# Reordering the set-up of a count-matrix build, and giving one half of an fp16 split to another engine

## The reference

```python
h = relu(layernorm(x)); x = x + L0(h)   # 4-head attention over the edges, segment sums by src
h = relu(layernorm(x)); x = x + L1(h)   # relu(h @ Wv + bv) * gamma, summed by dst
h = relu(layernorm(x)); x = x + L2(h)   # (h + pi * segment_sum(h[src], dst)) @ W.T + b
h = relu(layernorm(x)); x = x + L3(h)   # three Chebyshev filters, softmax mix, batch norm, relu
```

## Time and profile before

| | before |
|---|---|
| median of 3 runs | 1038.48 us (1036.12 to 1039.69) |
| profiled execution, own time | 1036.59 us |
| its span | 1034.8 us |
| mean granted TensorE clock | 0.973 |
| PE busy | 939.5 us (91%) |
| DVE busy | 855.0 us (83%) |
| ACT busy | 601.0 us (58%) |
| POOL busy | 530.0 us (51%) |

### The profile page before, as it was taken

How to read it: one execution, slowest core, us unless ns; L and a number is a source line. 1 busy time by engine, 2 the same in 40 slices (tenths; PEclk the granted TensorE clock), 3 DMA queues, 4 the chain that set the end, 5 groups by cost and what they waited for, 6 DMA issues and landing times.

```text
span 1034.8 us, 21453 instructions
## 1 busy us (share of the span) xinstructions
PE 939.5 (91%) x8293; PEld 563.3 (54%) x8293; DVE 855.0 (83%) x1296; ACT 601.0 (58%) x826; POOL 530.0 (51%) x522
## 2 busy tenths in 40 slices
PE   3787778888896999999999999999999999999995
PEld 2544445455462223232323333335699999999884
DVE  8899999999774999999999999999976745533466
ACT  8576677878546998989989898881100000001233
POOL 7788568575003999999999999870000000000000
PEclk9999998999896999999999999999999999999996
DMA  0010000000236122122222222230001100010211
GB/s 10 27 37 10 6 7 26 6 11 2 55 123 182 43 56 58 41 66 50 49 62 57 67 59 66 64 87 1 1 33 40 44 24 11 1 42 9 79 36 46
DMA packets 98577, 43.82 MB, mean 42 GB/s; under 512 B 85004, under 2 KB 96652, under 8 KB 98352
## 3 DMA queue, kind: packets, MB, share of 16 engines
q1 hardware_dynamic: 96784, 40.74, 15.0%
q0 software_dynamic: 1696, 1.74, 0.7%
HBM read 30.03 MB, written 12.41 MB: 41 GB/s over the span
## 4 chain that ended last, share of the span: by engine, by line
PE 66%; DVE 21%; issue 5%; ACT 3%; POOL 2%; DMA 2%; SPq 0%; DVEq 0%; ACTq 0%; POOLq 0%
PE PS L1322 20%; PE PS L1077 14%; PE PS L1087 12%; DVE oneS L410 7%; DVE mov L410 6%; PE PS L1820 4%; PE PS L1066 3%; PE PS L547 3%; PE PS L539 3%; ACT Eb L1134 2%; POOL Eb L977 1%; PE PS L1330 1%; PE PS L876 1%; DVE Eb L1151 1%; PE PS L1806 1%
## 5 line engine op out<-in xcount | busy, mean ns | idle before, releaser
L1151 DVE TENSOR_TENSOR Eb<-Eb,PS 128x2048 f32<-128x2048 f32 (+4 forms) x175 | 342.2, 2014 | 20.6 <-POOL Eb L977 10.6
L1134 ACT ACTIVATE Eb<-PS,small 128x1024 f32<-128x1024 f32 (+4 forms) x350 | 333.6, 1004 | 41.7 <-PE PS L1077 36.6
L977 POOL TENSOR_SCALAR Eb<-Eb 128x1024 f32<-128x1024 f32 (+4 forms) x350 | 318.9, 934 | 73.9 <-ACT Eb L1134 70.5
L1322 PE MATMUL PS<-hs,CT 128*128 128x192 f16 (+1 forms) x2500 | 212.5, 246 | 0.1
L583 ACT ACTIVATE CT<-PS 128x500 f32 x313 | 175.7, 586 | 62.7 <-PE PS L547 60.8
L1322 PEld LDWEIGHTS PS<-hs,CT 128*128 128x128 f16 (+1 forms) x2500 | 206.6, 98 | 3.2 <-issue 0.6
L1077 PE MATMUL PS<-Qb,Kb 96*128 96x512 f16 (+3 forms) x700 | 180.8, 362 | 9.7 <-DMA Kb<-kd 6.2
L1087 PE MATMUL PS<-Eb,V 128*25 128x512 f32 (+3 forms) x1400 | 167.5, 551 | 0.9 <-DVE Eb L1151 0.8
L539 PE MATMUL PS<-mov,oneS 128*128 128x100 f16 x1565 | 127.6, 214 | 40.0 <-DVE mov L410 31.8
L539 PEld LDWEIGHTS PS<-mov,oneS 128*128 128x128 f16 x1565 | 96.2, 101 | 97.8 <-DVE mov L410 52.4
L1077 PEld LDWEIGHTS PS<-Qb,Kb 96*128 96x128 f16 (+1 forms) x700 | 42.5, 98 | 195.4 <-ACT Eb L1134 185.3
(11 more groups left out here) (282 smaller groups left out, 904.3 us busy)
## 6 DMA issues: line engine op xcount, KB each, us to landing
Kb<-kd SPq DMA_DIRECT2D x168, 96.0 KB, 2.4
qd<-QH SPq DMA_DIRECT2D x12, 192.0 KB, 2.5
kd<-QH SPq DMA_DIRECT2D x12, 192.0 KB, 3.4
hs<-t_d SPq DMA_DIRECT2D x12, 192.0 KB, 2.5
Qb<-qd SPq DMA_DIRECT2D x4, 384.0 KB, 3.8
CT<-x_d SPq DMA_DIRECT2D x1, 1200.0 KB, 8.1
x_d<-B SPq DMA_DIRECT2D x6, 192.0 KB, 1.8
t_d<-A SPq DMA_DIRECT2D x6, 192.0 KB, 1.9
```

The lines of the kernel that those rows point to most:

```text
L977: g.tensor_scalar(e, e, EHI, ELO, ALU.min, ALU.max).then_inc(S("clamped"), 1)
L1134: a.activation(e, ps, ACT.Exp, scale=K.unsc[0:r, :]).then_inc(S("score_exp"), 1)
L1151: v.tensor_tensor(e, e, cn, ALU.mult).then_inc(S("weighed"), 1)
L1322: m = p.matmul(bank(t % FIRST)[0:r, 0:w], K.CT[:, a, 128 * t:128 * t + r], hs[:, a, :, :].rearrange("p k d -> p (k d)"), start=(a == 0), s ...
```

## The change

In the build: POOL no longer makes the slot numbers beyond the first block (L203 is gone). DVE makes them instead from the first 120 columns, by adding a constant (`more_slots`): for block 1 and blocks 2 to 3 ahead of the wait for `item0`, for blocks 4 to 7 behind `turnW`, for blocks 8 to 13 at set 1. `slots(0)` stands ahead of the `turnW` instructions. The zeros are shared anew: 1,800 and 9,000 columns on POOL, 6,500 on DVE, 14,500 and 7,550 on ACT. POOL's second piece stands ahead of `gather(1)`, and DVE's ahead of `slots(1)`. PE turns the first keys after the sums of blocks 1 to 3, ahead of those of blocks 4 to 7. The third part's comparisons move from sets 0 and 1 to sets 1 and 2, its sums from set 2 to set 3. `high(2)` moves from set 7 to set 5.

In L1: the high half is made by ACT, as a copy with a scale, behind `lin_copy(g + 1)` in its stream. The low half stays on DVE and moves out of `l1_d(g)` to behind `l1_a(g + 2)`.

```diff
-HIGH_AT = {3 if j == 1 else 6 * (j - 1) + 1: j for j in range(1, NJ)}
+HIGH_AT = {(3, 5)[j - 1] if j < 3 else 6 * (j - 1) + 1: j for j in range(1, NJ)}
...
-PAST_AT = {0: (0, 1, 2, 3), 1: (4, 5, 6)}
-SUM_AT, SLOTS_AT, TABLE_AT = 2, 5, 7
+PAST_AT = {1: (0, 1, 2, 3), 2: (4, 5, 6)}
+SUM_AT, SLOTS_AT, TABLE_AT = 3, 5, 7
...
-ZG1, ZG2 = 3500, 10500
-ZV = ZG2 + 4500
-ZA = ZV + 18500
+ZG1 = 1800
+ZG2 = ZG1 + 9000
+ZV = ZG2 + 6500
+ZA = ZV + 14500
+ZEROED = 5
...  build_gpsimd
-    g.iota(K.iotaS[:, BLOCK:SLOTS], [[GI, 12 * (NJ - 1)], [LH, 2], [1, GI]], base=GI * 12, channel_multiplier=0,
-           allow_small_or_imprecise_dtypes=True).then_inc(S("iota"), 1)
...
     keys(0)
+    g.memset(K.CTf[:, ZG1:ZG2], 0.0).then_inc(S("zero"), 1)
     g.wait_ge(S("slot_w"), 2)
     gather(1)
-    g.memset(K.CTf[:, ZG1:ZG2], 0.0).then_inc(S("zero"), 1)
...  build_vector
+    def more_slots(a, b):
+
+        v.wait_ge(step, own.n)
+        v.tensor_scalar(K.iotaS[:, BLOCK * a:BLOCK * b], K.iotaS[:, 0:BLOCK * (b - a)], float(12 * GI * a), None, ALU.add
+                        ).then_inc(step, own.up())
+
+    more_slots(1, 2)
+    more_slots(2, 4)
     v.wait_ge(S("item0"), 1)
...
         passes(0, t)
+    slots(0)
     v.wait_ge(S("identf"), 1)
...
-    slots(0)
-    v.wait_ge(S("iota"), 6)
+    K.turn_at = own.n
+    more_slots(4, 8)
     v.wait_ge(S("passed"), 1)
+    v.wait_ge(step, own.n)
...
     high(0)
+    v.memset(K.CTf[:, ZG2:ZV], 0.0).then_inc(S("zero"), 1)
     slots(1)
-    v.memset(K.CTf[:, ZG2:ZV], 0.0).then_inc(S("zero"), 1)
     table(0)
...
+        if s == 1:
+            more_slots(8, NJ)
+            v.wait_ge(step, own.n)
         if s in HIGH_AT:
...  build_tensor
     sums(0)
+    t.wait_ge(K.own["v"].sem, K.turn_at)
     windows(0)
-    sums(1)
+    sums(1, last=4)
     turn_items(0)
+    sums(1, first=4)
     windows(1)
...  prop_scalar
             lin_copy(g + 1, tiles(g + 1))
+        a.wait_ge(S("h2"), g + 1)
+        a.activation(K.HP[0][:, 4 * g:4 * g + tiles(g), 0, :], K.A[:, 4 * g:4 * g + tiles(g), :], ACT.Copy, scale=UP
+                     ).then_inc(S("hi"), 1)
...  prop_vector
-        v.wait_ge(S("h2"), g + 1)
-        split(A[:, 4 * g:4 * g + n, :], 0, g)
+
+    def l1_e(g):
+
+        n = tiles(g)
+        o = [K.HP[0][:, 4 * g:4 * g + n, i, :] for i in range(2)]
+        v.wait_ge(S("hi"), NJ + g + 1)
+        v.scalar_tensor_tensor(out=o[1], in0=A[:, 4 * g:4 * g + n, :], scalar=UP, in1=o[0], op0=ALU.mult, op1=ALU.subtract
+                               ).then_inc(S("split_l2"), 1)
...
         if g + 1 < NG:
             l1_a(g + 1)
+        if g:
+            l1_e(g - 1)
         l1_c(g)
         if g + 1 < NG:
             l1_b(g + 1)
         l1_d(g)
+    l1_e(NG - 1)
     degrees()
```

More of the change, by code:

```diff
@@ L425, in build_vector @@
     high(0)
+    v.memset(K.CTf[:, ZG2:ZV], 0.0).then_inc(S("zero"), 1)
     slots(1)
-    v.memset(K.CTf[:, ZG2:ZV], 0.0).then_inc(S("zero"), 1)
     table(0)
+    v.wait_ge(S("iota"), 5)
     soft = softmax_pieces(v, K)
@@ L483, in build_tensor, with sums @@
     t.matmul(bank(5)[0:BLOCK, 0:1], K.row0[:, :], K.onef[:, :], start=True, stop=True).then_inc(S("item0"), 1)
-    def sums(h):
+    def sums(h, first=0, last=NJ):
         a, b = PARTS[h]
-        for j in range(a, b):
+        for j in range(max(a, first), min(b, last)):
             for t_ in range(7):
@@ L492, in sums @@
                              start=(t_ == 0), stop=(t_ == 6))
-        m.then_inc(S("passed"), 1)
+        if b <= last:
+            m.then_inc(S("passed"), 1)
     def windows(h):
@@ L520, in build_tensor @@
     sums(0)
+    t.wait_ge(K.own["v"].sem, K.turn_at)
     windows(0)
-    sums(1)
+    sums(1, last=4)
     turn_items(0)
+    sums(1, first=4)
     windows(1)
     t.wait_ge(S("identb"), 1)
-    t.wait_ge(S("zero"), 5)
+    t.wait_ge(S("zero"), ZEROED)
     PE = mybir.EngineType.PE
@@ L576, in build_scalar @@
     a.activation(K.CTf[:, ZA:ZT], K.zf[:, 0:1].to_broadcast([128, ZT - ZA]), ACT.Copy).then_inc(S("zero"), 1)
-    a.wait_ge(S("zero"), 5)
+    a.wait_ge(S("zero"), ZEROED)
     for i, g in enumerate(PRESENT):
```

## The result

The changed kernel takes 1031.97 us (median of 5 runs, 1030.93 to 1032.83), the kernel before 1038.48 (5 runs, 1034.37 to 1039.69). The ratio is 0.9946, 95% interval 0.9933 to 0.9959: 5.6 us faster, between 4.3 and 7.0 (the two medians differ by 6.5). The forecast was 1030.4 within 1026.5 to 1034.5. In a second set of runs the same kernel had 1031.19 against 1038.53, ratio 0.9932 (0.9919 to 0.9946): 7.1 us, between 5.6 and 8.4.

A forecast was written before the change was run, and what follows sets the result against it. The prediction saw no single bound: PE carried 66% of the chain of waits, DVE 21%. Set-up 6.5 us plus L1 0.9 made 7.4 us, taken from a mean of 1037.7 for a forecast of 1030.4, range 1026.5 to 1034.5.

The forecast's parts named there:

- The head and the zeros: Set-up: without the iota and with zeros shared anew, PE's first set starts at 23.7 against 30.49, 6.8 us earlier.
- The 0.6 us that this would have cost here: Set-up head: by the skill's rule, more_slots held for POOL's short instructions would make the gain 0.6 us smaller.
- Sets 2 to 11: Build, stepped set by set: set 6 starts at 42.8 to 43.4 against 48.75, a gain of 5.4 to 5.9 us.
- my rival on the faster side: Set-up: the clock does not fall after the sums and fewer hold-ups spare the sets: 10 us, 1027.8; chance 0.10.
- The step that failed: Third block's keys before set 12: ready in time with high(2) at about 40, so DVE's wait goes: + 0.43 us.
- my first rival: Set-up's gain lost before set 12, by block 1's late keys among others: 4.2 us gain, 1033.5; chance 0.14.
- All sets alike from set 12 on: Build from set 12: nothing differs, and DVE's pace carries the 6.5 us lead to the build's end.
- my rival on the slower side: Build: PE's clock stays at the lower level, PE becomes the bound, net 10.3 us slower, 1048; chance 0.03.
- a lead that shrinks there: Sign of being wrong: the set-up's lead, forecast at 6.5 us, shrinks in the sets after 12.
- L1: High half moved to ACT closes PE's idle times at the second and fourth group: 0.39 + 0.52 = 0.9 us.
- One sign that I had named for being wrong: L1: ACT's new copy ends what DVE waits for; gain 0 if DVE waits each time as long as it saved.
- the 1.6 us slower stage: L1 priced by the longer ACT instruction alone, seven times 0.23 us: stage 1.6 us slower, whole gain 4.9.

The follow-up runs named there:

- Experiment 8: POOL's long iota replaced by DVE's additions alone, on the kernel before, with order and shares of zeros as before: 1033.59 us, ratio 0.9969.
- Experiment 11: The changed kernel with the old shares of zeros on POOL, DVE and ACT: 1030.43 us, ratio 0.9934 to the kernel before.
- experiment 5: The changed kernel with L1's high halves back on DVE, so the new set-up alone: 1031.62 us, ratio 0.9944 to the kernel before.
- Experiment 3: The changed kernel with POOL's keys(2) ahead of gather(3): 1028.66 us, ratio 0.9917 to the kernel before.
- Experiment 2: The changed kernel with high(2) back after set 7: 1031.74 us, ratio 0.9943 to the kernel before.
- experiment 4: The changed kernel with the third block's keys turned by PE after set 10 in place of set 9: 1029.69 us, ratio 0.9918 to the kernel before.
- experiment 6: L1's high halves on ACT alone, on the kernel before, with its build unchanged: 1035.79 us, ratio 0.9985.
- 10: The changed kernel with keys(2) ahead of gather(3) and high(2) back after set 7: 1029.56 us, ratio 0.9929 to the kernel before.
- 12: The changed kernel with one-element DVE memsets behind the one-hot instructions of sets 7 to 10: 1031.78 us, ratio 0.9948 to the kernel before.
- 7: high(2) after set 5 in place of set 7, alone, on the kernel before: 1036.41 us, ratio 0.9991.
- experiment 9: The changed kernel with keys(2) ahead of gather(3) and 22 more POOL comparisons from the fourth block on: 1030.44 us, ratio 0.9933 to the kernel before.

## Why the prediction was right, and where it was wrong

The total was right within its range: 7.4 us of gain forecast, 5.6 (4.3 to 7.0) measured in one set of runs and 7.1 (5.6 to 8.4) in the other. Part of that is luck. At set 6 the gain was larger than forecast (6.1 to 7.0 in three profiles, against 5.4 to 5.9), from there to set 12 the late keys took more back than forecast (3.4 to 6.3 left, against 6.5), and the two errors offset each other. (The sum itself is 0.1 off: 1037.7 less 7.4 is 1030.3.)

**The head and the zeros: right.** `lw` at 0.17 us, keys(0) ending at 14.34 (forecast 14.9), the last zeros at 22.05 (22.6), PE 1.08 us later at 23.13 (23.7). Experiment 8 shows the iota's part by itself: 4.83 us at `cI`. Experiment 11 shows that the last zeros, and not the one-hots, start PE. `lw` started at 2.96, before my own 3.3, since both `more_slots` (0.45 us together, from 1.89) fit into DVE's wait for `item0`. The Trainium skill (SBUF — State Buffer, Who interferes with whom) has a `tensor_scalar` in a two-port mode and a GpSimd instruction shut each other out. The 0.6 us that this would have cost here, by the prediction, did not come: POOL's short instructions, of 0.2 to 0.3 us, did not hold these two. The trace agrees with that rule at the comparisons of part 1. As forecast, they were held beside POOL's short memset: 4.87 us in place of 2.54, with their end at 11.46, where I had 11. It cost nothing here, and 1 us in experiment 8, where the long form of that memset stood in the way.

**Sets 2 to 11: the term was too small.** I forecast a gain of 5.4 to 5.9 at set 6; it was 7.0 and 6.6 in the two profiles of the changed kernel (6.1 in experiment 5). PE was ahead of my steps before its clock could matter: it began the sums at 35.83 and 35.90, where I had 36.6. What came behind them hung on the clock. In the first profile it did not fall (1.00 against 0.74 before), PE was soon through with sets 3 and 4 (their four groups start within 1.7 us each, 33.34 to 35.02 and 38.13 to 39.79), and set 6 waited 1.18 us, not about 2.3. From 38 to 44 us it was 0.72 in the second profile, with a wait of 1.93, and 0.50 in experiment 5. So the condition of my rival on the faster side, a clock that does not fall, held in one profile of three, and its 10 us came in none.

**The step that failed** is "With `high(2)` at about 40 the keys are there in time: + 0.43". high(2) was there, at 39.7, and the keys were not: PE waited 3.73 us for them, four times as long as before, then 2.38 in the second profile and 0.89, as before, in experiment 5. I had looked for what ended PE's wait of 0.89 in the chain before and found DVE's high part ahead of POOL's instructions; I had not added up POOL's own queue. Between the second and the third block's keys it holds two indirect DMAs (3.6 us) and seven instructions beside DVE's one-hots (14.3 us): 18 us for six sets that take DVE 16 to 17. Of the 14.3, 5.20 are the one held instruction; at the 1.13 of its median the keys would have ended at about 54.3 (an estimate from these rows), and PE, which came to them at 54.7, would not have waited. Such a hold was there before as well, behind a wait for high(2):
```profile
54.17 0.64 POOL L222 TENSOR_SCALAR key<-hi 120x128 f32<-120x128 int32 x1 [3.54 <-DVE hi L419]
54.89 5.11 POOL L224 TENSOR_TENSOR key<-dl,key 120x128 f32<-120x128 f32 x1
```
What the change moved is that DVE got its head start and POOL only part of it. The zeros of POOL end 7.5 us earlier (21.89 against 29.41), but `gather(1)`, which I had put behind them at no cost, takes 5.1 us there (22.07 to 27.19, its first issue alone 3.79), and the second block's keys begin only 2.6 us earlier (30.41 against 33.05). At the third block's keys the lead was 7.6 us on DVE's side (set 11) and 4.6 on POOL's, and POOL became the bound of that block. The term of + 0.43 stood for a wait of DVE that would go; that wait, ahead of set 12, was 4.47, 1.83 and, in experiment 5, 0.43 us. The lead at set 12 was 3.4, 5.3 and 6.3 in place of 6.5. Experiment 3 shows that POOL's queue is what PE waited for: with keys(2) first the wait is gone and the lead is 8.1. Whether the transfers ahead or the hold within counted for more, and what leaving `gather(1)` ahead of the zeros would have given, no run shows. Experiment 2 clears high(2) of it. This was my first rival in kind ("the late keys hold"), but I had placed it at block 1 and before set 6.

**All sets alike from set 12 on: nearly.** Up to set 79 the lead of the second profile goes from 5.3 to 4.9, experiment 3's from 8.1 to 7.4, experiment 4's from 6.5 to 6.0, experiment 8's from 3.5 to 3.6. In the first profile 1.6 us went (3.4 to 1.8), 0.9 of it at set 36, with the granted clock at 0.86. That is the mechanism of my rival on the slower side, in a size that decides nothing; the unchanged build of experiment 6 loses 0.7 us over the same sets against the profile before. By the words of the prediction a lead that shrinks there was a sign of being wrong; the 0.4 us of the second profile lie within that, the 0.9 at set 36 do not.

**L1: right.** 0.9 us forecast from PE's idle times, 1.02 measured (54.03 to 53.01), of which 0.81 are PE's idle time, and 1.34 in experiment 6. ACT's copy takes 0.52 us, longer than DVE's 0.36, and lies in ACT's idle time. One sign that I had named for being wrong did come: ACT's copy ended three of DVE's waits, 2.9 us in all. They cost nothing, since PE is the bound at that end of the stage; what I had wrong is that such a wait must matter. The Trainium skill (Perfetto Trace Analysis, Optimizing Scalar/DVE Operations) says that DVE is faster where it has a 2x or 4x mode; the copies' lengths agree (0.36 against 0.52), and the 1.6 us slower stage that I had priced by lengths alone did not come. It also says that unloading a saturated DVE may help. DVE was busy 49.36 of the 54.03 us, and the 1.02 us fit that.

**The levels.** The profiled execution before, at 1036.59, was among its faster ones, and the first one of the changed kernel, at 1032.83, the slowest of its five. From one set of runs to the next, the medians of before were 1038.5, 1038.5, 1037.3, 1037.0 and 1037.6. Part of that spread lies in the stretch from set 79 to the first attention score, which the change doesn't touch: 52.0 us before, 51.1 and 52.7 in the two profiles of the changed kernel, 50.3 to 53.1 in the others. This is why two profiles of one kernel differ by more than the terms that I was working out.

## What to carry to other kernels

When a stream is given a head start, add up every other engine's queue over the same stretch, DMAs and all, and ask whether that engine gets the head start too; the releaser of the old wait need not be what bounds that queue. A wait that ends in an engine's last instruction asks what stands in front of its first: here a transfer for the next block stood ahead of the keys that everyone needed. A copy moved from a full engine to an idle one is worth about the idle time of the bound engine that it closes (here 0.81 of 1.02 us), and not the instruction's length times its count. And take a mark from more than one profile before you explain it: three profiles of one build gave leads of 3.4, 5.3 and 6.3 us at set 12.

## What the runs showed of the hardware

DVE's instructions with a scalar operand were held beside POOL's iota and memsets: `lw` took 4.95 us and ended 0.03 us behind the iota; one comparison of about 0.43 us took 4.07 in the kernel before (beside the memset of 5.95), 3.87 in experiment 8 (3.03) and 2.43 after the change (1.61), and ended 0.2 us behind the memset each time. The last two began 0.6 us ahead of the memset, while POOL issued a transfer. DVE's own memset (6,500 columns in 5.47 us, as 4,500 in 3.81 before) and the one-hots were not slowed by POOL's memset of 7.61 us. The reverse hold was new to me: once, in sets 8 and 9, a POOL instruction of 0.5 us took 5.1 to 5.2, which is the length of four one-hot instructions of DVE. Of the 91 such instructions from 28 to 262 us in the first profile of the changed kernel, 48 took 1.25 to 1.95, about one one-hot instruction, six took 2.1 to 3.0, and two took longer (5.20 and 5.64). It came before the change (5.11), after it (5.20 and 5.19) and in experiments 2, 4, 5, 6, 8, 10, 11 and 12 (5.11 to 5.23), and was absent only in experiments 3, 7 and 9, where POOL was issuing DMAs in most of that stretch; in experiment 9 one of these took 4.79. A second one of 5.64 stands at about 150 us, after the change as before. The first comes behind `table(2)`, whichever POOL instruction is next. Twenty-two more POOL reads elsewhere cost DVE's pace nothing that shows (204.1 against 204.0 us). Why four in a row go ahead of POOL there was not found.

The granted clock around the third part's one-column matmuls differed between executions of the same build: from 38 to 44 us it was 1.00, 0.72 and 0.50 in three profiles.
